# Four pieces of the first patch chunk multiplied as a rounded part and a remainder, and buffers of dead tensors shared

## The reference

```
tokens = einsum('bpi,hi->bph', patches, W) + b          # 2352 -> 128
h = concat([cls, tokens]) * pos_embed
h = h + attention(layernorm(h))                         # softmax over the queries, causal
h = h + moe_top2_sigmoid(layernorm(h))                  # 32 experts, 128 -> 128 -> 128
h = h + decayed_context(layernorm(h))                   # cumulative sums, exponential decay
h = h + moe_top2_softmax(layernorm(h))                  # 16 experts, 128 -> 512 -> 128, GELU
```

## Time and profile before

| | |
|---|---|
| median of 3 runs | 1194.78 us (1192.02 to 1196.13) |
| profiled execution | 1194.46 us, span of its instructions 1192.7 us |
| mean granted TensorE clock | 0.881 |
| PE busy / DVE busy / ACT busy / POOL busy | 961.0 / 845.5 / 487.5 / 639.8 us |
| PE busy from 56 to 412 us (14 front steps) | 353.94 of 356.00 us |
| DVE, ACT busy in the same stretch | 281.99, 151.65 us |

### The profile page before, as it was taken

One profiled execution on the slowest core, in us unless ns is written; L12 is line 12 of the kernel. 1 busy time (PEld: TensorE's weight loads), 2 busy tenths in 40 slices (PEclk: granted clock), 3 DMA queues, 4 the chain that ended last, 5 costly groups with the idle time before them and its releaser, 6 DMA issues.

```text
span 1192.7 us, 21877 instructions
## 1 busy us (share of the span) xinstructions
PE 961.0 (81%) x6191; PEld 799.4 (67%) x6191; DVE 845.5 (71%) x3253; ACT 487.5 (41%) x1331; POOL 639.8 (54%) x638
## 2 busy tenths in 40 slices
PE   5999999999999951566677777666518999999995
PEld 2666766666766641465567676565418999999995
DVE  1478787778787753366666888776726888888885
ACT  1244444344443321111144434454505665655662
POOL 1015544455544444377754777777662555555554
PEclk9999999999999965689777977767757999999998
DMA  9856556656553004677887666445247777998893
GB/s 372 309 185 222 203 190 227 229 197 223 200 192 123 20 26 103 168 214 206 253 263 219 203 191 198 150 141 184 97 124 263 253 251 242 319 322 307 289 332 102
DMA packets 121048, 247.94 MB, mean 208 GB/s; under 512 B 21787, under 2 KB 88555, under 8 KB 114656
## 3 DMA queue, kind: packets, MB, share of 16 engines
q1 hardware_dynamic: 72768, 188.20, 47.9%
q0 software_dynamic: 19584, 34.70, 8.6%
q10 hardware_dynamic: 28576, 23.67, 6.7%
HBM read 203.03 MB, written 47.46 MB: 210 GB/s over the span
## 4 chain that ended last, share of the span: by engine, by line
PE 54%; DMA 15%; DVE 13%; POOL 6%; issue 5%; ACT 3%; SPq 2%; ACTq 1%; POOLq 0%; DVEq 0%
PE ps L828 11%; PE ps L810 9%; PE ps L652 8%; DMA xin<-lists_L 8%; PE ps L649 6%; POOL lists_L L1809 4%; POOL results_L L1823 3%; PE ps L791 3%; PE ps L713 3%; PE ps L697 2%; DMA results_L<-xin 2%; DVE ntok L1302 2%; PE ps L670 2%; PE ps L663 2%; DMA xrest<-in_x_rest 1%
## 5 line engine op out<-in xcount | busy, mean ns | idle before, releaser
L1809 POOL DMA_INDIRECT lists_L<-rows,slots x250 | 279.5, 1118 | 305.1 <-issue 300.6
L1823 POOL DMA_INDIRECT results_L<-xin x322 | 316.7, 983 | 224.8 <-DVE xin L1615 155.9
L828 PE MATMUL ps<-xin,hTb 128*128 128x128 f32 x1604 | 219.1, 286 | 5.5 <-DVE xin L1615 5.2
L828 PEld LDWEIGHTS ps<-xin,hTb 128*128 128x128 f32 x1604 | 204.9, 202 | 7.6 <-issue 7.4
L652 PE MATMUL ps<-xin,w_emb 128*128 128x512 f32 x384 | 182.0, 607 | 10.0 <-DMA w_emb<-in_w_main 10.0
L1121 ACT ACTIVATE hTb<-ps,xin 128x256 f32<-128x256 f32 x320 | 125.4, 475 | 106.9 <-PE ps L810 106.9
L791 PE MATMUL ps<-ident,xin 128*128 128x128 f32 x322 | 73.3, 314 | 99.5 <-DMA xin<-lists_L 98.9
L791 PEld LDWEIGHTS ps<-ident,xin 128*128 128x128 f32 x322 | 42.2, 157 | 111.6 <-DMA xin<-lists_L 111.3
L652 PEld LDWEIGHTS ps<-xin,w_emb 128*128 128x128 f32 x384 | 68.5, 194 | 68.9 <-issue 58.8
L1596 DVE TENSOR_SCALAR xin<-xin 128x128 f32<-128x128 f32 x322 | 101.8, 364 | 0.0
L810 PE MATMUL ps<-x_hi,x_lo 128*128 128x256 f32 x320 | 98.1, 307 | 0.0
(11 more groups left out here) (230 smaller groups left out, 2016.8 us busy)
## 6 DMA issues: line engine op xcount, KB each, us to landing
xin<-in_x_main SPq DMA_DIRECT2D x48, 1536.0 KB, 6.9
xin<-in_w_L SPq DMA_DIRECT2D x80, 578.0 KB
xin<-in_w_L SPq DMA_DIRECT2D x83, 128.0 KB
xin<-lists_L SPq DMA_DIRECT2D x80, 132.0 KB
xin<-in_w_L ACTq DMA_DIRECT2D x79, 128.0 KB
xin<-in_difference SPq DMA_DIRECT2D x13, 640.0 KB, 6.2
xin<-in_distance SPq DMA_DIRECT2D x13, 640.0 KB
x_hi<-results_L SPq DMA_DIRECT2D x11, 640.0 KB
```

The lines of the kernel that those rows point to most:

```text
L828: mm = pe.matmul(o, hTb[p2][:, f, q * 128:(q + 1) * 128], w2[:, f * D:(f + 1) * D], start=(f == 0), stop=(f == l.FC - 1))
L1809: pool.indirect_dma_start(out=lists[l.name], out_offset=bass.IndirectOffsetOnAxis(ap=slots_of(l, g, h)[:, t, k:k + 1], axis=0), in_=buf[:, ...
L1823: pool.indirect_dma_start(out=results[l.name], out_offset=bass.IndirectOffsetOnAxis(ap=xblk[u][:, q, PLACE:PLACE + 1].bitcast(U32), axis=0 ...
```

## The change

Four of the six tiles of chunk 0 (`KS = 4`) are embedded in the split form too, for groups 2 to 15 (`FIRST = 2`). There are single buffers `x_hi0`, `x_lo0` (128 x 2048) and weights `w_hi0`, `w_lo0` (128 x 512), made once. ACT's `high0(g+3)` stands behind the copy of `rows` and ahead of the exponentials in step g, DVE's `low0(g+3)` stands between `smax` and `lg`, for g = 0 to 12; those of group 2 stand ahead of step 0. PE waits for `split0` ahead of the first tile. To make room, `QT` and `KT`, `u0T` and `h1T`, and the two `x1T` become halves of `QK`, `UH` and `XT`; the block buffers `hTb` and `xTb` lie in `QK`, `UH` and `h0T`, and layer 1's `x2T` in `XT`. No instruction is added or removed by that.

```diff
+FIRST, KS = 2, 4
...
+        w_hi0, w_lo0 = sb("w_hi0", [128, KS, D], F32R), sb("w_lo0", [128, KS, D], F32R)
+        x_hi0, x_lo0 = sb("x_hi0", [128, KS, GP], F32R), sb("x_lo0", [128, KS, GP], F32R)
...
-        QT, KTt = sb("QT", [D, GT]), sb("KT", [D, GT])
+        XT = sb("XT", [D, 2 * GT])
+        x1T = [XT[:, h * GT:(h + 1) * GT] for h in range(2)]
+        QK, UH = sb("QK", [D, 2 * GT]), sb("UH", [D, 2 * GT])
+        QT, KTt = QK[:, 0:GT], QK[:, GT:]
...
-        xTb = [sb(f"xTb{h}", [D, 2 * 128]) for h in range(2)]
+        xTb = [h0T[h][:, :, :].rearrange("p i t -> p (i t)")[:, 0:2 * 128] for h in range(2)]
...
-        hTb = [sb(f"hTb{h}", [128, 4, 256]) for h in range(2)]
+        hTb = [both[:, 0:1024].rearrange("p (f n) -> p f n", f=4) for both in (QK, UH)]
...
+                        if c == 0 and g >= FIRST:
+                            pe.wait_ge(split0, g - FIRST + 1)
+                    if c == 0 and g >= FIRST and n < KS:
+                        for i, (w, x) in enumerate(((w_lo0, x_hi0), (w_hi0, x_lo0), (w_hi0, x_hi0))):
+                            mm = pe.matmul(psE[h], w[:, n, :], x[:, n, :], start=(n == 0 and i == 0), stop=False,
+                                           skip_group_check=True)
...
+            def high0(g, h, j):
+
+                act.wait_ge(chunk_in[h][0], 16 * (j + 1))
+                act.wait_ge(chunk_used[1 - h][0], j + h)
+                act.activation(x_hi0[:, :, :].rearrange("p k n -> p (k n)"),
+                               xin[h][0][:, 0:KS, :].rearrange("p k n -> p (k n)"), ACT.Copy).then_inc(x_hi0_ready, 1)
...
             high(0, 0, 0)
+            act.activation(w_hi0[:, :, :].rearrange("p k d -> p (k d)"),
+                           w_emb[:, 0:KS, :].rearrange("p k d -> p (k d)"), ACT.Copy).then_inc(w_hi_ready, 1)
...
                 r1_rows1(L0, g, h, j)
+                if FIRST <= g + 3 < GROUPS:
+                    high0(g + 3, 1 - h, (g + 3) // 2)
                 if ahead:
                     a4(g + 1, o, jo)
...
             for f in (a2, a3, a4):
                 f(0, 0, 0)
+            high0(2, 0, 1)
...
+            def low0(g, h):
+
+                dve.wait_ge(x_hi0_ready, g - FIRST + 1)
+                dve.tensor_tensor(x_lo0[:, :, :].rearrange("p k n -> p (k n)"),
+                                  xin[h][0][:, 0:KS, :].rearrange("p k n -> p (k n)"),
+                                  x_hi0[:, :, :].rearrange("p k n -> p (k n)").bitcast(F32), ALU.subtract)\
+                    .then_inc(split0, 1)
+
+            dve.wait_ge(w_hi_ready, 2)
+            dve.tensor_tensor(w_lo0[:, :, :].rearrange("p k d -> p (k d)"), w_emb[:, 0:KS, :].rearrange("p k d -> p (k d)"),
+                              w_hi0[:, :, :].rearrange("p k d -> p (k d)").bitcast(F32), ALU.subtract)
...
                     a3(g + 1, o, jo)
+                if g + 3 < GROUPS:
+                    low0(g + 3, 1 - h)
                 st = r2(L0, g, h, j)
...
             for f in (a2, a3, a4):
                 f(0, 0, 0)
+            low0(2, 0)
             e0(1, 1, 0)
```

More of the change, by code:

```diff
@@ L276, in build @@
         x_hi, x_lo = sb("x_hi", [128, KC, GP], F32R), sb("x_lo", [128, KC, GP], F32R)
+        w_hi0, w_lo0 = sb("w_hi0", [128, KS, D], F32R), sb("w_lo0", [128, KS, D], F32R)
+        x_hi0, x_lo0 = sb("x_hi0", [128, KS, GP], F32R), sb("x_lo0", [128, KS, GP], F32R)
         xrest = [sb(f"xrest{h}", [KREST, GP]) for h in range(2)]
         h0T = [sb(f"h0T{h}", [D, GI, SEQ]) for h in range(2)]
-        x1T = [sb(f"x1T{h}", [D, GT]) for h in range(2)]
-        QT, KTt = sb("QT", [D, GT]), sb("KT", [D, GT])
+        XT = sb("XT", [D, 2 * GT])
+        x1T = [XT[:, h * GT:(h + 1) * GT] for h in range(2)]
+        QK, UH = sb("QK", [D, 2 * GT]), sb("UH", [D, 2 * GT])
+        QT, KTt = QK[:, 0:GT], QK[:, GT:]
         V = [sb(f"V{h}", [SEQ, GI, D]) for h in range(2)]
@@ L285, in build @@
         ssum = sb("ssum", [SEQ, GI])
-        u0T = sb("u0T", [D, GT])
-        h1T = sb("h1T", [D, GT])
+        u0T, h1T = UH[:, 0:GT], UH[:, GT:]
         toks = [sb(n, [WIDE, TILES, D]) for n in ("atok", "ntok", "htok0", "htok1")]
@@ L296, in build @@
         rows = [r[0:ROWS] for r in rows_all]
-        x2T = {"L0": sb("x2T0", [D, TILES, ROWS]), "L1": sb("x2T1", [D, TILES, WIDE])}
+        x2T = {"L0": sb("x2T0", [D, TILES, ROWS]), "L1": XT[:, 0:TILES * WIDE].rearrange("p (t n) -> p t n", t=TILES)}
         slots = [sb(f"slots{h}", [128, TILES, TOP], U32) for h in range(3)]
@@ L398, in build @@
         split = sem("split")
+        x_hi0_ready, split0 = sem("x_hi0_ready"), sem("split0")
         consts_in = sem("consts_in")
@@ L646, in embed @@
                             pe.wait_ge(split, g + 2)
-                    if c == SPLIT:
+                        if c == 0 and g >= FIRST:
[4 more added lines that the diff above has]
+                                           skip_group_check=True)
+                    elif c == SPLIT:
                         for w, x in ((w_lo, x_hi), (w_hi, x_lo), (w_hi, x_hi)):
```

## The result

The changed kernel takes 1206.84 us, the median of 4 runs (1202.60 to 1207.12), against 1193.40 us for the kernel before (4 runs, 1189.83 to 1196.13). The ratio is 1.0105, with a 95% interval from 1.0077 to 1.0134: **slower by about 1%**, more than 1198.1, and outside the predicted range up to 1203.5. The profiled execution took 1202.60 us with a span of 1200.9 us, against 1194.46 and 1192.7.

A forecast was written before the change was run, and what follows sets the result against it. PE was taken to bound the front, busy 25.38 of 25.47 us a step. +3.9 +1.7 +2.6 -4.9 = +3.3 us took 1194.46 to 1197.8, or 1198.1 from the median; range 1195.0 to 1202.0, 8 in 10 1191.0 to 1203.5.

The forecast's parts named there:

- First split: Ahead of step 0: PE waits for group 2's rounding and subtraction, `b1` starts at 60.95 instead of 57.04, +3.9 us.
- Clock at the start: Behind PE's idle time ahead of step 0: 3.4 us at half speed, costing 1.7 us, taken once.
- My upper bound: Start of step 0: 3.9 us more if the clock returns only with tiles (4, 9), at most 5.6 us.
- `b1` 0.20 us later a step: Steps 1 to 13: 2.21 us of DVE subtraction against 2.01 us of slack, 13 x 0.20 = 2.6 us lost.
- Tiles (2, 4): Behind `b1`, ahead of the `h1T` transposes: shorter split tiles save 0.35 us a step, 14 x 0.35 = 4.9 us.
- The step before: Steady front step before the change: taken as 25.47 us, forecast 0.15 us shorter, 25.3 us.
- My sign that DVE decides more than `b1`: Steady front steps: the forecast is wrong in this way if they take over 25.5 us.
- PE keeps everything: Front steps: `pick` does not move `b1`, all 9.8 us come back, -3.8 us net, 1191.0; chance 0.12.
- The clock falls in the steady steps: PE's 0.55 us idle time ahead of `b1`: half of 13 steps lose 1.7 us each, +11, 1209; chance 0.09.
- Seams cost: At each `b2`: a float32 matmul behind a split one costs 0.19 us, 14 x 0.19 = 2.7, 1200.8; chance 0.13.
- No stall: Ahead of step 0: group 2's split is ready in time or its wait is absorbed, 1192.1; chance 0.05.
- Back-to-back issue gap: Split matmuls on PE: at 216 ns each a pair saves 0.43 us, the sum 1.1 us less, 1197.0.

The follow-up runs named there:

- the repetition: The changed kernel, unaltered, measured once more: 1201.09 us, ratio 1.0076 to the kernel before.
- ACT's and DVE's part alone: Changed kernel with all splits made, group 2's ahead of `a2`, but PE multiplying chunk 0 in float32: 1195.95 us, ratio 1.0045 to the kernel before.
- group 2 early: Changed kernel with group 2's rounding right behind `a2(0)` and its subtraction right behind `low(1)`: 1193.15 us, ratio 1.0012 to the kernel before.
- the steps' splits early: Changed kernel with each step's rounding between `a2` and `a3` and subtraction behind `low`: 1194.03 us, ratio 1.0025 to the kernel before.
- PE's part alone: Changed kernel with only group 2 split, ahead of `a2`; later groups multiply its old split values: 1181.17 us, ratio 0.9940 to the kernel before.
- the shared buffers alone: Changed kernel with shared buffers and split weights kept, but no tile of chunk 0 split: 1192.41 us, ratio 1.0014 to the kernel before.
- the five added matmuls: Changed kernel with five unread float32 matmuls of 128x512 on PE ahead of step 0: 1197.36 us, ratio 1.0055 to the kernel before.
- both moves: Changed kernel with group 2's split and the steps' splits both moved earlier: 1183.26 us, ratio 0.9944 to the kernel before.

## Why the prediction was wrong

The direction was right, the size was not: 3.3 us forecast, 9.6 measured at the end of the front. The medians lie further apart, 13.4 us in the first measurement and 11.0 in the repetition; what the steps below explain is the 9.6 us of the profile. The profiled execution, 1202.60 us, lies inside the range up to 1203.5, the median of 1206.84 does not. By the steps of the sum:

- **First split, 3.9 us.** Measured 3.83, with `low0` at 57.18 to 59.47 and PE at 59.62, as worked out (57.2, 59.5, 59.6). Right.
- **Clock at the start, 1.7 us ("I take this once").** This is **the step that failed**: 5.06 us. I took the length of the half clock from the early fall, where 3.4 us of it follow a gap of 2.46 us. Here it lasted for 10.8 us of unbroken work. My upper bound, "3.9 more if it comes back only with the dense tiles (4, 9)", with 5.6 at most, is what happened: `b1`, the short pairs and the transposes ran to their end at half speed, and the clock rose at 70.46 us, just behind the start of tiles (4, 9). Nearly the whole of what is computed between the gap and those tiles is paid for twice (5.68 us at full speed, 10.69 here). I held the bound in the range's working but let it reach to 1202.0 alone.
- **`b1` 0.20 us later a step.** From the first matmul of the last split chunk to `b1` it is 7.80 us before (202.51 to 210.31) and 8.03 after (211.17 to 219.20): 0.23. ACT's and DVE's part alone makes the whole step 0.22 us longer, the 0.07 of the next but one point among it. Right.
- **Tiles (2, 4), 0.35 us back a step.** The way from the first transposes behind `b1` to the second ones went from 2.26 to 1.93 us (221.01 to 222.94), 0.33. Right.
- **What the step left out.** `b1` itself now takes 1.81 us from start to start (219.20 to 221.01) instead of 1.74, and its row says 1.97 instead of 1.90. It is 1.97 where `b1` starts on `pick` (the changed kernel, group 2 early, ACT's and DVE's part alone), and 1.90 where it does not (the steps' splits early, PE's part alone). So the wait costs 0.07 us more than its length. +0.23 + 0.07 - 0.33 is -0.03 a step where I had -0.15.
- **The step before, 25.47 us.** It is one of the shorter ones; the mean is 25.52, because `ntok` takes 1.50 us in seven steps of ten and not 1.43. In the changed kernel it takes 1.50 in nearly every step. So steps are 25.51 instead of the forecast 25.3, and 12 of them gave 0.08 us more instead of 1.8 less. My sign that DVE decides more than `b1`, steps over 25.5 us, was set from the short step and says nothing: the kernel before is over it too.
- **Step 14** was not in the sum: there the clock was low in both kernels, it came back later in the changed one, and that took 0.84 us. The kernel with the shared buffers alone lost 1.24 us there, so this is no effect of the split that any run shows; why the time differs is open.

Together: from step 0 8.84 us where I had 5.25 (3.9 + 1.7 - 0.35), from the steps 0.08 for -1.8, from the last steps 0.65 for -0.15. This is 9.57 for 3.3. The 8.84 us are 3.83, 5.06 and -0.35, and 0.30 more; of these 0.21 are that the first split matmul starts at 59.62 in the changed kernel and at 59.41 in the one with the five added matmuls, from which the 3.83 are taken.

**The rivals.** *PE keeps everything* did not come true as the change stands: `pick` moves `b1`, and the first split stalls. With both splits moved forward it is what the chip does, 0.9944. *The clock falls in the steady steps*: it did not, the granted clock is 1.00 through them with 13 waits of 0.27 us. The rule of the Trainium skill, page "TensorE: Matmul & The Clock Gate", section "Why this matters for your kernels", that it takes idle gaps of microseconds, agrees with these steps and not with step 14, where the kernel before went to half clock at 414.98 us and 0.74 us had preceded it. *Seams cost*: nothing, by the 24.77 us of PE's part alone. *No stall*: the stall was there as forecast; moved away, the kernel takes 1.0012 of the time before, which is no change. The pace of the split matmuls was 0.229 us, as in the earlier trace rows, and the saving of a pair came out at 0.35; with the 216 ns of the Trainium skill, page "TensorE: Matmul & The Clock Gate", section "Back-to-back issue gap", it would have been 0.43, and no run shows that.

**What stays open.** What decides how long the half clock lasts: the work behind the early wait and behind the stall differ (below), but no run changes that work alone. Each run of the changed kernel in the first measurement but the profiled one is 4 us longer than that one (1206.84 to 1207.12 against 1202.60), and none of these has a trace; the repetition has its median at 1201.09. One step, from 354.11 to 379.89, takes 25.78 us; the kernel with group 2's split early has one as well (344.68 to 370.48, 25.80). Why `ntok` lasts 1.38, 1.43 or 1.50 us is not settled: it differs between the steps of the kernel before too.

## What to carry to other kernels

Price a stall of PE together with the work behind it: here that went at half clock for 10.8 us, and this cost more of the front (5.1 us) than the stall itself (3.8 us). Do not take the length of one half clock for that of another, and keep the upper bound as a case of its own with a chance. Idle time of an engine is cover only where it lies: the same 2.2 us of DVE work cost 0.2 us a step between `smax` and `lg`, and nothing behind `low`, where DVE would have waited for PE. Before a change is dropped because it does not pay, look for its two or three late instructions; moving them turned +1.0% (+0.8% in the repetition) into -0.6%.

## What the runs showed of the hardware

- **The clock's return.** After 4.24 us of idle time it took 10.8 us of work without a gap (the short pairs, `b1`, transposes, the first of the tiles (4, 9)) until the clock was at 2.4 GHz again. After 2.46 us at 25.79 it was 3.4 us of half clock, with eighteen split matmuls of 512 columns behind it, and in two other profiles (shared buffers alone, PE's part alone), where that wait is recorded as 3.46 and 3.08 us, the clock stayed at 1.00.
- **The same stall, three moments of the fall, one of the return.** In the three profiles with the stall of some 4.2 us the clock fell at 56.9 us, with PE idle, in the changed kernel, and at 61.5 (its repetition) and 60.1 us (the steps' splits earlier), when PE was back at work already. In all three it rose 0.15 to 0.25 us after the tiles (4, 9) began (70.46, 71.66 and 70.26 us). Such tiles are not needed for it: in step 14 of the kernel before it rose at 428.6 us, among transposes. No run shows what decides.
- **A wait ahead of a group of matmuls costs more than its length.** The sixteen matmuls of `b1` take 0.07 us more where their start hangs on `pick` (1.97 for 1.90).
- **The issue of an indirect transfer on POOL is held up by a long subtraction on DVE.** The timeline of POOL in the kernel before, where DVE's `x_lo` of 3072 columns runs from 221.37 to 224.72:

```profile
220.92 0.99 POOL L1809 DMA_INDIRECT lists_L<-rows,slots  x1 [0.30 <-issue]
222.22 3.37 POOL L1809 DMA_INDIRECT lists_L<-rows,slots  x1 [0.30 <-issue]
```

and in the kernel with both moves, where the two subtractions run back to back from 216.34 to 221.89:

```profile
215.30 1.00 POOL L1849 DMA_INDIRECT lists_L<-rows,slots  x1 [0.30 <-issue]
216.60 6.16 POOL L1849 DMA_INDIRECT lists_L<-rows,slots  x1 [0.30 <-issue]
```

It ends 0.87 us after DVE is done. So it is with each of the 13 subtractions of 3072 columns in the kernel before that have such an issue beside them (0.85 to 0.88 us), and with each pair in the kernel with both moves. PE waits for none of these in the steps. That an expert block which needs such a transfer would see the delay is an inference; no run shows it.
